# Expert composites from weights split into two FP32R parts: three products in place of one FP32 product, for seven of eight experts

## The chip, the cores and the metric

The kernel runs on one core of a Trainium2 chip. The metric is the device time of one execution, in microseconds (us); smaller is better. TensorE is PE in the rows, VectorE is DVE, ScalarE is ACT, GpSimd is POOL, and SyncE, which issues most DMAs, is SP.

## The reference

The input x has 4 batches of 1024 tokens with 256 features. With xn = layernorm(x):

```python
Q = (x @ Wq.T).reshape(H, b, s, dkh)      # H = 16, dkh = 16; K and V alike
atten = softmax(einsum('hbqd,hbkd->hbqk', Q, K))
out = einsum('hbqk,hbkd->hbqd', atten, V).reshape(b, s, -1)
y = out + x                               # normalised over (1, 2) of each batch
...
logits = xt @ w_gate.T                    # top 2 of 8 experts, softmax of the two
for e in range(E):
    h = xt @ w_in[e].T
    y = y + gates[:, e:e + 1] * (h @ w_out[e].T)
```

The result is x + attention(xn) + experts(xn). There is no nonlinearity between the two products of an expert, so w_out[e] @ w_in[e] can be multiplied first, as one 256x256 matrix. All inputs and the output are FP32.

## The kernel before

Everything is unrolled, each engine has one instruction stream written out by hand, and streams meet only at counting semaphores.

**Composites (first 84 us).** For each of the eight experts `expert_product` (L952) builds the composite matrix of 256x256 from the weights, in two half steps s = 0, 1 of 512 hidden units each. I number the half steps i = 2e + s, from 0 to 15. A half step takes 1 MB of weights: a slot `win[i % 6]` (w_in, 128 partitions x 1024) and a slot `wout[i % 6]` (w_out transposed, the same size). It makes eight products of a 128x128 stationary block with 256 moving columns (two blocks `dh` of the output by four blocks `h` of hidden units) in plain FP32 (L960). The sum stands in PSUM; when both halves of an expert are in, ScalarE (`m_out`, L482) rounds it to FP32R (`mth`) and VectorE (`m_lo`, L667) takes the rest (`mtl`). TensorE may begin expert e only when `m_lo(e - 2)` is done, as banks alternate.

**Work between the composites.** The 32 tiles of tokens come in eight chunks of four tiles. For chunks 0 and 1 TensorE transposes the normalised tokens (`transposes`, L915), and projects values with gate logits (`project_v`, L936) and queries and keys (`project_qk`, L925), in the order of L968 to L993: half steps 0 and 1, transposes(0), half step 2, four `project_v`, two `project_qk`, half step 3, two `project_qk`, half step 4, transposes(1), half step 5, four `project_v`, half step 6, two `project_qk`, half step 7, two `project_qk`, and half steps 8 to 15 with nothing between them. These products already run on operands split in two FP32R parts, three products each. ScalarE empties banks (`xt_out` L489, `v_out` L497, `qk_copy` L517), VectorE takes rests (`xt_lo`, `qk_lo_half`) and computes statistics, GpSimd raises to the power -1/2 (`scale_of_chunk`, L394).

**Loads.** SP issues in one queue (L305 to L320): `load_weights` (L278) for half step i waits until TensorE is done with half step i - 6, whose slot it takes. Ahead of half step 10 stands `qk_out(0)`, eight stores. Slots 2 to 5 are memory that later holds tokens of chunks 4 to 7, so those tokens are loaded after the composites of experts 0 to 5.

**After the composites.** TensorE waits for all sixteen `m_lo` (L1012) and then computes, tile after tile, the products of tokens with composites (`y_bank`, L995), with the rest of the projections between; from about 280 us on the attention follows, up to 985 us, and a short end.

Of the kernel before, what the change touches and what calls it, by code (L numbers as in the profile page):

```python
# [4 lines left out]
FP32 = mybir.dt.float32  # L5
FP32R = mybir.dt.float32r
BF16 = mybir.dt.bfloat16
ALU = mybir.AluOpType
# [3 lines left out]
P = 128  # L12
# [3 lines left out]
def attention_and_experts(nc, x, wq_t, wk_t, wv_t, wg_t, w_in, w_out_t, out):  # L16
    BATCH, S, D = x.shape
# [26 lines left out]
    AHEAD = 8  # L44
    PAIR = 2
    HELD = 4
    SETS = 3
    BY_VECTOR = E // 4

# [8 lines left out]
    with ctx:  # L58
        def sb(name, shape, dt=FP32):
            return ctx.enter_context(nc.sbuf_tensor(name, shape, dt))  # L60

        def sem(name, n=None):
            if n is None:
                return ctx.enter_context(nc.semaphore(name))
            return [ctx.enter_context(nc.semaphore(f"{name}{i}")) for i in range(n)]
# [48 lines left out]
        win = [r.rearrange("p (h d) -> p h d", h=HU) for r in room[0::2]]  # L114
        wout = [r.rearrange("p (h d) -> p h d", h=HU) for r in room[1::2]]
        WS = len(win)
        vb = sb("vb", [P, 2, NKT, VW])
        weights = [picks[:].rearrange("p i t e -> p (i t e)"), vstage[:].rearrange("p t o k v -> p (t o k v)")[:, 0:POS]]
        weights += [wp[:, i, :] for i in (3, 0, 1, 2)]
# [51 lines left out]
        gates_done = sem("gates_done")  # L171
        w_in_s = sem("w_in_s", WS)
        half_done = sem("half_done")
        m_ready = sem("m_ready")
        mh_done = sem("mh_done")
        ml_done = sem("ml_done")
# [96 lines left out]
        def _(sp):  # L273
# [4 lines left out]
            def load_weights(e, s):  # L278

                i = 2 * e + s  # L280
                slot, earlier = i % WS, i - WS
                if earlier >= 0:
                    sp.wait_ge(*((m_ready, KT * (earlier // 2 + 1)) if earlier % 2 else (half_done, earlier // 2 + 1)))
                rows = slice(e * HID + s * HU * P, e * HID + (s + 1) * HU * P)
                for half, w in ((win, w_in), (wout, w_out_t)):
                    sp.dma_start(half[slot], w.rearrange("e h d -> (e h) d")[rows, :]
                                 .rearrange("(p h) d -> p h d", h=HU)).then_inc(w_in_s[slot], 16)
# [94 lines left out]
        def _(pool):  # L382
# [6 lines left out]
            nc.gpsimd.affine_select(out=ident[:], in_=ident[:], compare_op=ALU.not_equal, fill=1.0,  # L389
                                    base=0, pattern=[[-1, P]], channel_multiplier=1).then_inc(const_step, 1)  # L390

            nc.gpsimd.memset(kf[:].bitcast(FP32), 1.0).then_inc(att_const, 1)

            def scale_of_chunk(c):  # L394
                pool.wait_ge(mv_done, 2 * (c + 1))
                nc.gpsimd.tensor_tensor(veps[:], var[:], epst[:, 0:TC], ALU.add).then_inc(veps_done, 1)
                pool.wait_ge(veps_done, c + 1)
                nc.gpsimd.tensor_tensor(rstd[:], veps[:], mhalf[:, 0:TC], ALU.pow).then_inc(rstd_done, 1)

            for c in range(NC // 2):  # L400
                scale_of_chunk(c)

            def add_scaled(t):
                tile = acc[:, bass.ds(t, 1), :].rearrange("p o d -> p (o d)")
# [71 lines left out]
        def _(act):  # L476
# [2 lines left out]
            nc.scalar.copy(wvgh[:], wvg).then_inc(w_hi, 1)  # L479
            nc.scalar.copy(wqkh[:], wqk).then_inc(w_hi, 1)  # L480

            def m_out(e):  # L482

                for dh in range(KT):
                    act.wait_ge(m_ready, KT * e + dh + 1)
                    nc.scalar.copy(mth[:, dh, bass.ds(e, 1), :].rearrange("p o d -> p (o d)"),
                                   ps[:, M_BANK[e % 2][dh], 0:D]).then_inc(mh_done, 1)

            def xt_out(c):  # L489

                if c >= SETS:
                    act.wait_ge(y_ready[-1], TC * (c - SETS + 1))
                for kt in range(KT):
                    act.wait_ge(xt_psum, KT * c + kt + 1)
                    nc.scalar.copy(xth[:, c % SETS, kt, :], ps[:, XT_BANK[kt], :]).then_inc(xth_done, 1)

            def v_out(c, t):  # L497

                if t == 0:
                    act.wait_ge(ones_done, 1)  # L500
                    act.wait_ge(v_stored, 16 * c)
                act.wait_ge(project_ready, 2 * TC * c + t + 1)
                bank = PROJECT_BANK[t % 2]
                nc.scalar.copy(lg[:, TC * c + t, :], ps[:, bank, D:D + E]).then_inc(v_evac, 1)
                nc.scalar.copy(vstage[:, t, :, :, 0:DH], ps[:, bank, 0:D]
                               .rearrange("p (k o d) -> p o k d", o=2, d=DH)).then_inc(v_evac, 1)
                if t == TC - 1:
                    act.wait_ge(v_evac, 2 * TC * (c + 1))
                    act.dma_start(v_d[c * CH:(c + 1) * CH].rearrange("(t p) o f -> p t (o f)", p=P),
                                  vstage[:].rearrange("p t o k v -> p t (o k v)")).then_inc(v_stored, 16)  # L510

            def second_weight(pair):
                act.wait_ge(gap_done, pair + 1)
                rows = slice(PAIR * TC * pair, PAIR * TC * (pair + 1))
                nc.scalar.activation(ex[:, rows], gap[:, rows], ACT.Exp).then_inc(gexp_done, 1)

            def qk_copy(c, o):  # L517
                if o == 0:
                    act.wait_ge(qk_stored, 128 * c)
                act.wait_ge(project_ready, 2 * TC * c + TC + o + 1)  # L520
                nc.scalar.copy(stage[:, 0, o, :].bitcast(FP32R), ps[:, PROJECT_BANK[o % 2], :]).then_inc(qk_hi, 1)  # L521
# [14 lines left out]
                                         ).then_inc(ff_scaled[j - BY_VECTOR], 1)  # L536

            xt_out(0)
            m_out(0)
            for t in range(TC):  # L540
                v_out(0, t)
            for o in range(2):
                qk_copy(0, o)
            m_out(1)
            for o in range(2, 4):
                qk_copy(0, o)
            xt_out(1)
            m_out(2)
            for t in range(TC):
                v_out(1, t)  # L550
            for o in range(2):
                qk_copy(1, o)
            m_out(3)
            for o in range(2, 4):
                qk_copy(1, o)
            m_out(4)
            second_weight(0)
            for e in range(5, E):
                m_out(e)

            for t in range(NT - 1):
                c, i = t // TC + PAIR, t % TC
# [63 lines left out]
        def _(dve):  # L626
# [31 lines left out]
            def xt_lo(c):  # L658

                if c >= SETS:  # L660
                    dve.wait_ge(y_ready[-1], TC * (c - SETS + 1))
                for kt in range(KT):
                    dve.wait_ge(xth_done, KT * c + kt + 1)
                    nc.vector.tensor_tensor(xtl[:, c % SETS, kt, :], ps[:, XT_BANK[kt], :],
                                            xth[:, c % SETS, kt, :].bitcast(FP32), ALU.subtract).then_inc(xtl_done, 1)

            def m_lo(e):  # L667

# [33 lines left out]
            def first_choice(pair):  # L702
                rows = slice(PAIR * TC * pair, PAIR * TC * (pair + 1))
                dve.wait_ge(v_evac, 2 * TC * PAIR * (pair + 1))
                pick(rows, lg, top1, oh1)
# [70 lines left out]
            nc.vector.tensor_tensor(wvgl[:], wvg, wvgh[:].bitcast(FP32), ALU.subtract).then_inc(w_lo, 1)  # L776
            nc.vector.tensor_tensor(wqkl[:], wqk, wqkh[:].bitcast(FP32), ALU.subtract).then_inc(w_lo, 1)
            xt_lo(0)
            m_lo(0)
            token_statistics(1)  # L780
            normalise_tokens(1)
            for o in range(2):
                qk_lo_half(0, o)
            m_lo(1)
            for o in range(2, 4):
                qk_lo_half(0, o)
            xt_lo(1)
            m_lo(2)
            token_statistics(2)
            normalise_tokens(2)  # L790
            for o in range(2):
                qk_lo_half(1, o)
            m_lo(3)
            for o in range(2, 4):
                qk_lo_half(1, o)
            dve.wait_ge(const_step, 6 + E)
            first_choice(0)
            second_choice(0)
            m_lo(4)
            gate_weights(0)  # L800
            token_statistics(3)
            normalise_tokens(3)
            for e in range(5, E):
                m_lo(e)

            for t in range(NT - 1):
                c, i = t // TC + PAIR, t % TC
# [106 lines left out]
        def _(pe):  # L914
# [36 lines left out]

            def expert_product(e, s):  # L952

                slot = (2 * e + s) % WS
                pe.wait_ge(w_in_s[slot], 32 * ((2 * e + s) // WS + 1))
                for dh in range(KT):
                    if s == 0 and e >= 2:
                        pe.wait_ge(ml_done, KT * (e - 2) + dh + 1)
                    for h in range(HU):
                        last = nc.tensor.matmul(ps[:, M_BANK[e % 2][dh], 0:D], win[slot][:, h, dh * P:(dh + 1) * P],  # L960
                                                wout[slot][:, h, :], start=s == 0 and h == 0,
                                                stop=s == 1 and h == HU - 1)
                    if s == 1:
                        last.then_inc(m_ready, 1)
                    elif dh == KT - 1:
                        last.then_inc(half_done, 1)
# [222 lines left out]
```

## Time and profile before

| | us |
|---|---|
| median of three runs | 1004.07 (1003.32 to 1004.2) |
| the profiled execution: its time | 1001.28 |
| its span, first to last instruction | 999.5 |
| PE busy / DVE / ACT / POOL in the span | 974.0 / 780.2 / 694.2 / 285.1 |
| first y product of the second part begins at about | 85.3 |

The span is cut into 40 slices of 25 us in the page; the change touches the first four. A matmul's end is modelled, so what a product costs is read from the distance between starts, not from its duration. The instructions of the change run in the first 85 us; every engine but TensorE is below 60% busy there.

### The profile page before, as it was taken

The page shows a single profiled execution, that of the slowest core. Times are in us where ns is not written, and L with a number is a line of the kernel's source. Part 1 is how long each engine was busy: PE and PEld are TensorE (multiplying, and loading weights), DVE is VectorE, ACT ScalarE, POOL GpSimd, SP SyncE. Part 2 cuts the span into 40 slices and gives each one's busy share as a digit, 9 for nine tenths or more (in the row PEclk, how much of TensorE's full clock was granted, in tenths as well). Part 3 has the DMA queues.
Part 4 walks back from the last instruction along what each step waited for, and adds up shares of the span by engine and source line. Part 5 has one row for each costly group of instructions (what it writes and reads, how often), then busy time and mean ns, then how long its engine had stood idle before and what let it go on. Part 6 is the DMA issues. An engine that isn't in the chain of part 4 may idle for free.

```text
span 999.5 us, 20786 instructions
## 1 busy us (share of the span) xinstructions
PE 974.0 (97%) x7816; PEld 504.5 (50%) x7816; DVE 780.2 (78%) x961; ACT 694.2 (69%) x1385; POOL 285.1 (29%) x389
## 2 busy tenths in 40 slices
PE   7999999999998999999999999999999999999994
PEld 6888888888876433333333333333333333333332
DVE  4344454543466899999999999999999999999975
ACT  2312333333322789999989899898989999899994
POOL 2001445544455222223222322223222322223222
PEclk9999999999999999999999999999999999999997
DMA  9967442223200133333333333333333333332204
GB/s 355 366 248 217 144 139 76 72 78 107 88 23 1 43 98 92 97 92 95 92 93 95 88 100 87 97 92 93 94 91 99 86 98 92 95 93 73 73 23 162
DMA packets 127043, 108.59 MB, mean 109 GB/s; under 512 B 81120, under 2 KB 102368, under 8 KB 126944
## 3 DMA queue, kind: packets, MB, share of 16 engines
q1 hardware_dynamic: 122720, 102.81, 35.4%
q10 hardware_dynamic: 4224, 4.46, 1.3%
q8 instruction: 62, 1.02, 0.4%
q14 instruction: 37, 0.30, 0.1%
HBM read 80.75 MB, written 42.21 MB: 123 GB/s over the span
## 4 chain that ended last, share of the span: by engine, by line
PE 96%; POOL 1%; DMA 1%; DVE 1%; issue 1%; ACT 0%; DVEq 0%; SPq 0%; ACTq 0%; POOLq 0%
PE ps L1081 28%; PE ps L1061 22%; PE ps L1007 18%; PE ps L1039 11%; PE ps L960 6%; PE ps L932 4%; PE ps L948 2%; PE ps L1097 1%; PE ps L1109 1%; PE ps L921 1%; DMA wp<-w_out_t 0%; DMA qf<-ot 0%; POOL rden L425 0%; ACT stage L534 0%; DVE xn L885 0%
## 5 line engine op out<-in xcount | busy, mean ns | idle before, releaser
L750 DVE TENSOR_REDUCE negm<-ps 128x1 f32<-128x1024 f32 x512 | 614.8, 1222 | 31.7 <-PE ps L1039 27.3
L585 ACT ACTIVATE wp<-ps 128x512 f32<-128x512 f32 x680 | 368.9, 595 | 43.7 <-PE ps L1061 6.7
L1061 PE MATMUL ps<-qf,kf 50*128 50x512 f32 x1024 | 373.1, 446 | 0.1
L1039 PE MATMUL ps<-kf,qf 48*128 48x512 f32 x1024 | 366.1, 444 | 1.0 <-DVE negm L750 1.0
L1061 PEld LDWEIGHTS ps<-qf,kf 50*128 50x128 f32 x1024 | 152.6, 185 | 199.0 <-ACT wp L585 97.5
L1081 PE MATMUL ps<-wp,vb 128*17 128x256 f32 x2720 | 212.6, 385 | 0.1
L1039 PEld LDWEIGHTS ps<-kf,qf 48*128 48x128 f32 x1024 | 147.2, 185 | 4.3 <-issue 3.9
L425 POOL TENSOR_TENSOR rden<-choice,minus 128x16 f32<-128x16 f32 x31 | 90.3, 2914 | 151.5 <-ACT choice L604 151.5
L585 ACT ACTIVATE picks<-ps 128x512 f32<-128x512 f32 x172 | 102.7, 597 | 22.8 <-PE ps L1061 5.0
L741 DVE SCALAR_TENSOR_TENSOR acc<-ps,gates,acc 128x256 f32<-128x256 f32 x64 | 30.8, 482 | 101.3 <-PE ps L1007 97.2
L1081 PEld LDWEIGHTS ps<-wp,vb 128*17 128x17 f32 x2720 | 46.0, 95 | 122.7 <-ACT vstage L585 53.2
L440 POOL TENSOR_TENSOR mpart<-negm,zero 128x8 fp32r<-128x8 f32 x64 | 12.9, 201 | 321.3 <-DVE negm L750 321.3
L1007 PE MATMUL ps<-mth,xth 128*128 128x512 f32 x256 | 102.6, 401 | 1.2 <-DVE stage L739 0.5
L585 ACT ACTIVATE vstage<-ps 128x512 f32<-128x512 f32 x172 | 101.8, 592 | 1.1 <-PE ps L1061 1.1
L1007 PE MATMUL ps<-mth,xtl 128*128 128x512 f32 x256 | 101.0, 395 | 0.0
L1007 PE MATMUL ps<-mtl,xth 128*128 128x512 f32 x256 | 100.9, 394 | 0.0
L534 ACT ACTIVATE wp<-ps,gates 128x256 f32<-128x256 f32 x96 | 40.3, 471 | 51.1 <-PE ps L1007 51.1
L521 ACT CAST stage<-ps 128x512 fp32r<-128x512 f32 x32 | 18.8, 587 | 60.2 <-PE ps L932 51.2
L1007 PEld LDWEIGHTS ps<-mth,xth 128*128 128x128 f32 x256 | 48.1, 188 | 14.4 <-issue 4.8
L1081 PE MATMUL ps<-picks,vb 128*17 128x256 f32 x688 | 53.9, 385 | 0.9 <-issue 0.8
L408 POOL TENSOR_TENSOR wp<-wp 128x512 f32<-128x512 f32 x24 | 31.1, 1294 | 82.8 <-ACT wp L534 82.8
L1007 PEld LDWEIGHTS ps<-mth,xtl 128*128 128x128 f32 x256 | 48.1, 188 | 11.5
(124 smaller groups left out, 898.9 us busy)
## 6 DMA issues: line engine op xcount, KB each, us to landing
qk_d<-stage SPq DMA_DIRECT2D x64, 256.0 KB
feat_d<-qk_d SPq DMA_DIRECT2D x64, 256.0 KB, 3.3
qf<-feat_d SPq DMA_DIRECT2D x128, 128.0 KB
qf<-feat_d SPq DMA_DIRECT2D x128, 64.0 KB
kf<-feat_d SPq DMA_DIRECT2D x128, 64.0 KB
v_d<-vstage ACTq DMA_DIRECT2D x8, 544.0 KB, 4.8
vb<-v_d SPq DMA_DIRECT2D x128, 34.0 KB, 2.4
acc<-x SPq DMA_DIRECT2D x8, 512.0 KB, 7.2
```

The costliest lines, as they stand in the source:

```text
L408: nc.gpsimd.tensor_tensor(scaled[:, 0:2], scaled[:, 0:2], scaled[:, 2:4], ALU.add).then_inc(ff_step, 1)
L425: nc.gpsimd.tensor_tensor(rden[:], rows[:, :, :, DH], minus[:], ALU.pow).then_inc(rows_step, 1)
L534: nc.scalar.activation(sums_of(t)[0][:, 2 * (j - BY_VECTOR) + h, :], ps[:, y_bank_of(t, j), h * D:(h + 1) * D], ACT.Copy, scale=gates[:, t ...
L585: nc.scalar.activation(weight_tile(n, j, b)[:, h * HALF:(h + 1) * HALF], ps[:, score_bank(score_turn[unit, b]), :], ACT.Exp).then_inc(exp_ ...
L741: nc.vector.scalar_tensor_tensor(out=total, in0=product, scalar=gate, in1=total, op0=ALU.mult, op1=ALU.add).then_inc(ff_added[j], 1)
L750: nc.vector.tensor_reduce(negm[:, n % 2, qt:qt + 1], ps[:, b:b + 2, :].rearrange("p b c -> p (b c)"), AX.X, ALU.max, negate=True).then_inc ...
L932: last = nc.tensor.matmul(ps[:, PROJECT_BANK[o % 2], :], w[:, o // 2, kt, (o % 2) * P:(o % 2 + 1) * P], v[:, c % SETS, kt, :], start=i == ...
L960: last = nc.tensor.matmul(ps[:, M_BANK[e % 2][dh], 0:D], win[slot][:, h, dh * P:(dh + 1) * P], wout[slot][:, h, :], start=s == 0 and h == ...
L1007: last = nc.tensor.matmul(ps[:, y_bank_of(t, j), :], v[:, t // TC % SETS, kt, tokens], m[:, kt, 2 * j:2 * j + 2, :].rearrange("p e d -> p ...
L1039: last = nc.tensor.matmul(ps[:, MAX_BANK[turn % 2] + half, :], qf[rows, u, qt * P:(qt + 1) * P], kf[rows, u, :], start=True, stop=True)
L1061: nc.tensor.matmul(ps[:, score_bank(score_turn[unit, half]), :], kf[rows, u, j * P:(j + 1) * P], qf[rows, u, h * HALF:(h + 1) * HALF], sta ...
L1081: last = nc.tensor.matmul(ps[32 * c:32 * c + VW, PV_BANK, 0:POS // 4], vb[:, n % 2, j + b * NKT // 2, :], weight_tile(n, j, b)[:, c * (POS ...
```

## The change

Half steps 2 to 15 no longer multiply in FP32. ScalarE rounds both weight slots of a half step to FP32R (`high_of_weights`), GpSimd subtracts the rounded w_in from w_in (`low_of_w_in`), VectorE does so for w_out (`low_of_w_out`). TensorE makes three FP32R products for each one before (high by high, high by low, low by high), 24 in a half step. The split parts stand in two buffers that alternate: `split[0]` is `qf`, `split[1]` is `kf` and the third set of `xth` and `xtl`. So the rounding for half step i waits until TensorE is done with i - 2. A weight slot comes free when its rests are taken. Half steps 0 and 1 stay in FP32. GpSimd's memset of `kf` moves behind the composites. VectorE's statistics of chunk 3, its gate work and its `m_lo` are put in another order, as is GpSimd's `scale_of_chunk`.

```diff
+        flat_kf = kf[:].rearrange("p s k -> p (s k)")
+        split = [[qf[:, i, :] for i in range(4)],
+                 [flat_kf[:, 0:POS], flat_kf[:, POS:2 * POS], xth[:, SETS - 1].rearrange("p k t -> p (k t)"),
+                  xtl[:, SETS - 1].rearrange("p k t -> p (k t)")]]
...
-                if earlier >= 0:
-                    sp.wait_ge(*((m_ready, KT * (earlier // 2 + 1)) if earlier % 2 else (half_done, earlier // 2 + 1)))
+                if 0 <= earlier < WHOLE:
+                    sp.wait_ge(*((m_ready, KT) if earlier else (half_done, 1)))
+                elif earlier > 0:
+                    sp.wait_ge(w_in_low, earlier - WHOLE + 1)
+                    sp.wait_ge(w_out_low, earlier - WHOLE + 1)
...
-            nc.gpsimd.memset(kf[:].bitcast(FP32), 1.0).then_inc(att_const, 1)
...
-            for c in range(NC // 2):
-                scale_of_chunk(c)
+            def low_of_w_in(i):
+                pool.wait_ge(w_high, 2 * (i - WHOLE) + 1)
+                high, low = split[i % 2][0:2]
+                nc.gpsimd.tensor_tensor(low, win[i % WS], high.bitcast(FP32), ALU.subtract).then_inc(w_in_low, 1)
+            scaled_after = {0: 0, 2: 1, 6: 2, 9: 3}
+            for i in range(2 * E):
+                if i >= WHOLE:
+                    low_of_w_in(i)
+                if i in scaled_after:
+                    scale_of_chunk(scaled_after[i])
+            pool.wait_ge(m_ready, KT * E)
+            nc.gpsimd.memset(kf[:].bitcast(FP32), 1.0).then_inc(att_const, 1)
...
+            def high_of_weights(i):
+                slot = i % WS
+                act.wait_ge(w_in_s[slot], 32 * (i // WS + 1))
+                if i >= WHOLE + 2:
+                    act.wait_ge(*((m_ready, KT * ((i - 2) // 2 + 1)) if i % 2 else (half_done, (i - 2) // 2 + 1)))
+                nc.scalar.copy(split[i % 2][0], win[slot]).then_inc(w_high, 1)
+                nc.scalar.copy(split[i % 2][2], wout[slot]).then_inc(w_high, 1)
...
             xt_out(0)
+            high_of_weights(2)
             m_out(0)
             for t in range(TC):
                 v_out(0, t)
+            high_of_weights(3)
             for o in range(2):
                 qk_copy(0, o)
+            high_of_weights(4)
             m_out(1)
             for o in range(2, 4):
                 qk_copy(0, o)
+            high_of_weights(5)
             xt_out(1)
+            high_of_weights(6)
             m_out(2)
             for t in range(TC):
                 v_out(1, t)
+            high_of_weights(7)
...
+            high_of_weights(9)
+            high_of_weights(10)
             m_out(4)
-            second_weight(0)
             for e in range(5, E):
+                high_of_weights(2 * e + 1)
+                if e + 1 < E:
+                    high_of_weights(2 * e + 2)
                 m_out(e)
+                if e == E - 2:
+                    second_weight(0)
...
+            def low_of_w_out(i):
+                dve.wait_ge(w_high, 2 * (i - WHOLE) + 2)
+                high, low = split[i % 2][2:4]
+                nc.vector.tensor_tensor(low, wout[i % WS], high.bitcast(FP32), ALU.subtract).then_inc(w_out_low, 1)
...
+            low_of_w_out(9)
             dve.wait_ge(const_step, 6 + E)
+            token_statistics(3)
+            low_of_w_out(10)
+            m_lo(4)
+            normalise_tokens(3)
+            low_of_w_out(11)
             first_choice(0)
+            low_of_w_out(12)
+            m_lo(5)
             second_choice(0)
-            m_lo(4)
+            low_of_w_out(13)
+            low_of_w_out(14)
+            m_lo(6)
+            low_of_w_out(15)
             gate_weights(0)
-            token_statistics(3)
-            normalise_tokens(3)
-            for e in range(5, E):
-                m_lo(e)
+            m_lo(7)
...
-                slot = (2 * e + s) % WS
-                pe.wait_ge(w_in_s[slot], 32 * ((2 * e + s) // WS + 1))
+                i = 2 * e + s
+                if i < WHOLE:
+                    pe.wait_ge(w_in_s[i], 32)
+                    products = [(win[i], wout[i], h) for h in range(HU)]
+                else:
+                    pe.wait_ge(w_in_low, i - WHOLE + 1)
+                    pe.wait_ge(w_out_low, i - WHOLE + 1)
+                    in_high, in_low, out_high, out_low = split[i % 2]
+                    products = [(a, b, h) for h in range(HU) for a, b in ((in_high, out_high), (in_high, out_low), (in_low, out_high))]
```

The lines left out of VectorE's order put `low_of_w_out(2)` to `(8)` at the places at which ScalarE's order has `high_of_weights(2)` to `(8)`.

## Rows read from the trace of the kernel before

**Rows 1.** The page: busy tenths and granted clock in 40 slices, and the chain by engine.
```profile
PE   7999999999998999999999999999999999999994
...
PEclk9999999999999999999999999999999999999997
...
PE 96%; POOL 1%; DMA 1%; DVE 1%; issue 1%; ACT 0%; DVEq 0%; SPq 0%; ACTq 0%; POOLq 0%
```
**Rows 2.** The chain of waits in order of time, 0 to 100 us: start, us, what.
```profile
6.09 10.02 PE ps L960 x32
...
16.98 3.46 PE ps L960 x16
20.43 3.07 PE ps L948 x24
...
26.36 3.45 PE ps L960 x16
...
55.93 27.64 PE ps L960 x128
...
84.48 1.09 PE ps L921 x8
```
**Rows 3.** Timeline of TensorE, 20 to 24 us: start, us, engine, line, what.
```profile
20.39 0.28 PE L948 MATMUL ps<-wvgl,xth 128*128 128x264 f32 x1
...
21.60 0.28 PE L948 MATMUL ps<-wvgh,xtl 128*128 128x264 f32 x1
```
**Rows 4.** Groups by line and form, 0 to 280 us: busy, mean ns | idle before.
```profile
L408 POOL TENSOR_TENSOR wp<-wp 128x512 f32<-128x512 f32 x24 | 31.1, 1294 | 82.8 <-ACT wp L534 82.8
...
L410 POOL TENSOR_TENSOR wp<-wp 128x256 f32<-128x256 f32 x24 | 17.8, 740 | 1.9
...
L486 ACT CAST mth<-ps 128x256 fp32r<-128x256 f32 x16 | 5.9, 376 | 31.8 <-PE ps L960 31.8
...
L777 DVE TENSOR_TENSOR wqkl<-stage,wqkh 128x1024 fp32r<-128x1024 f32 x1 | 1.2, 1219 | 0.0
L480 ACT CAST wqkh<-stage 128x1024 fp32r<-128x1024 f32 x1 | 1.0, 1040 | 0.0
```
**Rows 5.** Timelines: the tail of the kernel, then 96 to 98 us.
```profile
993.71 0.69 DVE L911 TENSOR_TENSOR stage<-xn,acc 128x512 f32<-128x512 f32 x1
994.08 1.44 POOL L472 TENSOR_TENSOR stage<-xn,acc 128x512 f32<-128x512 f32 x1 [1.19 <-ACT xn L622]
...
994.67 2.00 DVE L911 TENSOR_TENSOR stage<-xn,acc 128x512 f32<-128x512 f32 x2 [0.28 <-ACT xn L622]
...
96.26 1.80 DVE L654 TENSOR_SCALAR xn<-acc,mean,rstd 128x256 f32<-128x256 f32 x4
96.42 0.85 POOL L416 TENSOR_TENSOR acc<-acc,wp 128x256 f32<-128x256 f32 x1
```
**Rows 6.** Lines L911 and L654 alone: duration ns min/median/max.
```profile
L911 DVE TENSOR_TENSOR stage<-xn,acc x3: 678/691/1396, 993.7 to 996.0; 128x512 f32<-128x512 f32 x3
...
L654 DVE TENSOR_SCALAR xn<-acc,mean,rstd x32: 400/407/869, 11.2 to 192.8; 128x256 f32<-128x256 f32 x32
```
**Rows 7.** Timeline of ScalarE at 16 us, of VectorE and GpSimd at 65 us.
```profile
16.58 1.07 ACT L495 CAST xth<-ps 128x512 fp32r<-128x512 f32 x2 [5.26 <-PE ps L921]
...
65.03 1.41 DVE L633 BATCH_NORM_STATS2 st<-acc 128x6 f32<-128x256 f32 x4
...
67.61 1.01 POOL L398 TENSOR_TENSOR rstd<-veps,mhalf 128x4 f32<-128x4 f32 x1
```
**Rows 8.** Timeline of SP's DMA issues, 29 to 40 us: the eight of `qk_out(0)`.
```profile
30.69 8.44 SPq L293 DMA_DIRECT2D qk_d<-stage  x8
```
**Rows 9.** Windows, and PE's last products: us, PE, PEld, DVE, ACT, POOL busy, PEclk, DMA share, GB/s.
```profile
6.09:12.38 6.29, 6.29 (x16) 4.92 (x16) 3.34 (x14) 1.58 (x2) 1.22 (x2) 1.00 1.05 377
...
988.00:989.00 1.00, 0.00 (x0) 0.00 (x0) 0.28 (x1) 0.00 (x0) 0.64 (x1) 0.50 0.44 155
...
984.74 0.66 PE L1097 MATMUL ps<-ident,ot 128*128 128x128 f32 x4 [0.49 <-ACT ot L597]
```

More of the change, by code:

```diff
@@ L46, in attention_and_experts @@
     HELD = 4
+    WHOLE = 2
     SETS = 3
@@ L116, in attention_and_experts @@
         WS = len(win)
+        flat_kf = kf[:].rearrange("p s k -> p (s k)")
+        split = [[qf[:, i, :] for i in range(4)],
+                 [flat_kf[:, 0:POS], flat_kf[:, POS:2 * POS], xth[:, SETS - 1].rearrange("p k t -> p (k t)"),
+                  xtl[:, SETS - 1].rearrange("p k t -> p (k t)")]]
+        split = [[part.rearrange("p (h d) -> p h d", h=HU) for part in parts] for parts in split]
         vb = sb("vb", [P, 2, NKT, VW])
@@ L173, in attention_and_experts @@
         half_done = sem("half_done")
+        w_high = sem("w_high")
+        w_in_low = sem("w_in_low")
+        w_out_low = sem("w_out_low")
         m_ready = sem("m_ready")
@@ L492, in xt_out @@
                     act.wait_ge(y_ready[-1], TC * (c - SETS + 1))
+                elif c == SETS - 1:
+                    act.wait_ge(m_ready, KT * E)
                 for kt in range(KT):
@@ L550, in _ @@
                 v_out(1, t)
+            high_of_weights(7)
             for o in range(2):
                 qk_copy(1, o)
+            high_of_weights(8)
             m_out(3)
@@ L778, in _ @@
             xt_lo(0)
+            low_of_w_out(2)
             m_lo(0)
@@ L781, in _ @@
             normalise_tokens(1)
+            low_of_w_out(3)
             for o in range(2):
                 qk_lo_half(0, o)
+            low_of_w_out(4)
             m_lo(1)
@@ L786, in _ @@
                 qk_lo_half(0, o)
+            low_of_w_out(5)
             xt_lo(1)
+            low_of_w_out(6)
             m_lo(2)
@@ L790, in _ @@
             normalise_tokens(2)
+            low_of_w_out(7)
             for o in range(2):
                 qk_lo_half(1, o)
+            low_of_w_out(8)
             m_lo(3)
@@ L958, in expert_product @@
                         pe.wait_ge(ml_done, KT * (e - 2) + dh + 1)
[L959 to L962, printed above, removed]
+                    for k, (a, b, h) in enumerate(products):
+                        last = nc.tensor.matmul(ps[:, M_BANK[e % 2][dh], 0:D], a[:, h, dh * P:(dh + 1) * P], b[:, h, :],
+                                                start=s == 0 and k == 0, stop=s == 1 and k == len(products) - 1)
                     if s == 1:
```

## The prediction

> **What bounds the kernel now.** I read the page first: TensorE is 90% busy or more in nearly every slice and at full granted clock, and the chain that ends last runs over it for 96% of the span [rows 1]. The chain in order of time shows the part that the change touches: from 6.09 us on TensorE hands over to itself, without a gap, until the composites are done and 84.48 begins the next part [rows 2]. So up to 84.48 us whatever TensorE gains or loses moves the end of the kernel, and since what follows is again bound by TensorE [rows 1], the shift is kept to the end. The question is one number: when does the product at 84.48 start after the change?
>
> **What the change removes.** Eight half steps without anything between them take 27.64 us [rows 2], 3.455 us each. The new half step has 24 FP32R products of 256 columns. The rows have 264 columns: ten starts from 20.39 to 21.60 [rows 3], 0.121 us apiece, so 256/264 of it is 0.1174 and the half step 2.82 us. That is 0.64 us less, fourteen times: **-8.9 us**, if TensorE never waits.
>
> **What it adds, by instruction.** Each of 14 half steps gets two roundings of 128x1024 on ScalarE, 1.04 us each [rows 4], the second begins about 0.93 after the first (two casts of one line overlap by about a tenth [rows 7]); a rest of 128x1024 on VectorE, 1.22 [rows 4]; and one on GpSimd, for which no row has the size. Its 128x256 takes 0.740 and its 128x512 1.294 [rows 4], so 0.554 per 256 more and 1.294 + 2 x 0.554 = **2.40** (I use 2.41). Bounds: 2.2 if the slope falls, 2.6 if twice the 512 row. In busy time this is little: 29 us on ScalarE, 17 on VectorE, 34 on GpSimd, in 80 us. What counts is that they stand in a row before TensorE may start.
>
> **The latency of one half step.** Count from the start of the first rounding. Alone: 1.04, GpSimd 2.41, handoffs 0.1: TensorE may start after **3.55** (VectorE would be done at 1.97 + 1.22, earlier). But the two rests overlap, and both read two SBUF tensors. What that costs shows once in the trace: the L911 that starts at 994.67, while GpSimd's L472 of the same kind runs until 995.52, takes 1.396 instead of 0.691 [rows 5, 6]. It loses 0.705 of an overlap of 0.85, so it goes at 0.16 of its pace, and GpSimd takes 1.44 instead of 1.29, about 0.85 of its pace. The second place agrees in kind: an L654 took 0.869 for 0.407 beside L416 [rows 5, 6]. In the new half step GpSimd starts at 1.07, VectorE at 2.00. GpSimd has 1.48 left, at 0.85 of its pace 1.74, and ends at 3.74; VectorE has done 0.16 x 1.74 = 0.28 by then, its 0.94 left end at 4.68. TensorE starts at **4.72**. I take this value, because its rows are the same instruction on the same engines; 3.55 stays as the lower end.
>
> The Trainium skill, page "GPSIMD Engine Reference", section "Key points", says that GpSimd shares its SBUF interfaces with VectorE, with contention where a VectorE instruction has two SBUF inputs. It gives no size; by it alone the latency would lie somewhere above 3.55.
>
> **The sum, half step by half step.** I went through the four written orders with these durations: a half step starts when TensorE is free and its rests are taken; its rounding when ScalarE is free and half step i - 2 is done. The starts, before and after:
> - Half step 2 was started at 16.98 [rows 2], right behind the transposes. Now ScalarE first rounds the transposes (1.07 from 16.58 [rows 7]), then the weights: 17.65 to 18.1 + 4.72 = 22.8. **+5.8**. Behind it, in TensorE's order, stand the projections of chunk 0, and all that hangs on them.
> - Half step 3: 26.36 before [rows 2]. Its rounding stands behind the last `v_out`, at 29.7, and its VectorE rest has not ended when GpSimd begins the rest of half step 4, whose rounding is free to follow at once. So VectorE is slowed twice over and ends at 36.7. **+10.3**.
> - Half steps 4 to 8 have projections between them (3.07 us for four of `project_v` [rows 2]), which cover most of the latency: the deficit stays between 9.4 and 10.8.
> - Half step 9: +11.3. Half step 10: +14.0, since GpSimd's queue has `scale_of_chunk(3)` ahead of rest 10, and that waits for VectorE's statistics, which now stand behind rest 9; from their start to the end of the power is 65.03 to 68.62 [rows 7], 3.6 us.
> - From half step 11 on nothing is between. An odd half step's rounding waits for the end of half step i - 2 (start + 2.98) and for `m_out` of its second block (0.28 more; one cast is 0.376 [rows 4]). Then 4.72 and 0.1 for the restart: 8.1 us a pair against 6.91 before, +1.2 a pair, half step 15 at 96.9 against 80.1, and the product of 84.48 at 100.7: **+16.2**. The saving of 8.9 is within this sum; it is paid back wholly, as each of the fourteen steps waits for a latency longer than the product it follows.
>
> **The clock.** Two of the waits are long, 5 us each (before half steps 2 and 3). At the tail, TensorE's last products start at 984.74, and in the slice 988 to 989 the granted clock is 0.50, 1.2 GHz [rows 9]. And a start after idleness is dear: the first 16 records take 6.3 us [rows 9] against 3.455 for later ones [rows 2], though the column shows 1.00 there. So after each long wait up to 2.8 us may be lost: 0 to 5.6, I take 3, since part would fall in waits that are there anyway. Together +19.2.
>
> **What costs nothing.** SP's loads: a slot comes free with the rests, and the eight stores of `qk_out(0)`, 8.44 us of issue [rows 8], stand ahead of half step 10 as before; its weights are issued at about 41, by my walk, and needed at 68, so they have over 20 us. The memset of `kf` comes as TensorE starts a part in which `kf` isn't read. If the latency were gone, loads would be next, not now.
>
> The profiled execution took 1001.28, the median is 1004.07; the shift is added to the median: 1004.07 + 19.2 = **1023** rounded.
>
> **The rivals.**
> 1. *The rests don't hinder each other here* (latency 3.55). For it: one wholly overlapped instruction is thin evidence. Against: both rows of it agree. The same walk gives 89.2 for the product of 84.48, +4.7, and one long wait at the clock's price, +0 to 2.8: **1009 to 1012**. Chance 0.17.
> 2. *TensorE is slowed all over*: pauses of 2 to 3 us between products of 2.8 keep the granted clock at 1.2 GHz for stretches. The tail shows that level after a pause [rows 9]; nothing shows it after pauses this short. Another 5 to 10 us: **1028 to 1035**. Chance 0.15.
> 3. *Faster.* The latency hides behind the other half step. Place: the start of odd half steps. A pair costs 3.4 plus the latency, and TensorE needs 5.65, so it decides at a latency of 2.2 us, less than GpSimd's instruction alone; it would need that rest to take about 1.1, as VectorE's does. Then only the wait at half step 2 is left, some 4.4, against 8.9 gained: **999.5**. Chance 0.06.
> 4. *A wash*: rival 1 with a GpSimd of about 1.8 us; within 2 us of before, **1002 to 1006**. Chance 0.05.
>
> The forecast itself, contention as measured and the clock lost at most at two places, has 0.57. The range 1008 to 1032 leaves out faster, wash and the far half of rival 2, about 2 in 10. The least that a measurement of this kernel tells from no change is about 0.2%, 2 us: faster by more 0.06, within it 0.05, slower 0.89.
>
> **What would show it.** In the profile after: FP32R products of L960's successor spaced 0.117 us (right or wrong on the saving); a TensorE wait of over 4 us before half step 2 and before half step 3, released by VectorE's rest; GpSimd's 128x1024 at 2.4 to 2.8; VectorE's rest of 1.22 alone stretched to 2.5 and more in most of 14 cases; pairs of 8.1 us at the end of the composites; the first y product near 101 to 105 instead of 85. The forecast is wrong if VectorE's rest stays at 1.2 (rival 1), if the granted clock shows 0.50 beyond the first 45 us (rival 2), or if TensorE's waits sum to less than 9 us (rivals 3 and 4).

## The result and the profile after

The changed kernel takes 1026.36 us (1025.83 to 1027.25) against 1003.7 of the kernel before on the same chip: ratio **1.0227**, 95% interval 1.0209 to 1.0244, 22.7 us slower. The profiled executions are 1026.5 and 1001.28, 25.2 apart, as the one of before was among its quickest.

The page of the changed kernel, busy tenths and granted clock in 40 slices, and the chain by engine; these answer to [rows 1]:

```profile
PE   4887999999999999999999999999999999999994
...
PEclk9998999999999999999999999999999999999997
...
PE 88%; DVE 3%; DMA 2%; ACT 2%; POOL 1%; issue 1%; SPq 1%; DVEq 0%; ACTq 0%; POOLq 0%
```

All that differs is in the first slices. The chain of waits in order of time (start, us, what) answers to [rows 2]; L1034 is the product that was L960, L510 and L511 are ScalarE's roundings, L717 is VectorE's rest, L414 GpSimd's, L988 the transposes that open the second part:

```profile
17.12 1.07 ACT xth L528 x2
18.20 0.94 ACT qf L510
19.14 0.95 ACT qf L511
20.12 2.54 DVE qf L717
22.79 5.46 PE ps L1034 x24
...
34.73 2.48 DVE xtl L717
37.34 3.12 PE ps L1034 x24
...
79.05 4.65 PE ps L1034 x24
...
98.59 0.94 ACT kf L510
99.53 0.95 ACT xth L511
100.51 2.56 DVE xtl L717
103.21 4.62 PE ps L1034 x24
...
108.73 1.09 PE ps L988 x8
```

Before, the chain through this part was TensorE handing over to itself. Now it goes ScalarE, ScalarE, VectorE, TensorE, again and again, and the transposes that began at 84.48 [rows 2] begin at 108.73, **24.25 us later**. That is nearly the whole of the loss: of the 25.2 us by which the spans differ only 0.95 arise after it.

Starts of the half steps in the trace, and how far each is behind the kernel before:

| half step | before | after | behind | forecast behind, clock apart |
|---|---|---|---|---|
| 2 | 16.98 | 22.79 | 5.8 | 5.8 |
| 3 | 26.36 | 37.34 | 11.0 | 10.3 |
| 8 | 55.93 | 67.0 | 11.1 | 9.4 to 10.8 |
| 9 | 59.4 | 72.41 | 13.0 | 11.3 |
| 10 | 62.8 | 79.05 | 16.2 | 14.0 |
| 15 | 80.1 | 103.21 | 23.1 | 16.8 |
| second part | 84.48 | 108.73 | 24.25 | 16.2 |

**The rests.** VectorE's and GpSimd's instructions in order of time (start, us, engine, what; in brackets the wait before):

```profile
20.12 2.52 DVE L717 TENSOR_TENSOR qf<-xn,qf 128x1024 fp32r<-128x1024 f32 x1 [1.09 <-ACT qf L511]
...
34.73 2.47 DVE L717 TENSOR_TENSOR xtl<-xn,xth 128x1024 fp32r<-128x1024 f32 x1 [6.51 <-ACT xth L511]
...
38.32 2.21 DVE L717 TENSOR_TENSOR qf<-acc,qf 128x1024 fp32r<-128x1024 f32 x1
...
59.88 1.22 DVE L717 TENSOR_TENSOR xtl<-wp,xth 128x1024 fp32r<-128x1024 f32 x1
...
74.31 1.22 DVE L717 TENSOR_TENSOR qf<-acc,qf 128x1024 fp32r<-128x1024 f32 x1
...
88.95 1.75 DVE L761 SCALAR_TENSOR_TENSOR picks<-picks,choice 128x64 f32<-128x64 f32 x1
...
92.11 1.22 DVE L717 TENSOR_TENSOR xtl<-wp,xth 128x1024 fp32r<-128x1024 f32 x1
93.69 2.96 DVE L717 TENSOR_TENSOR qf<-xn,qf 128x1024 fp32r<-128x1024 f32 x1 [0.36 <-ACT qf L511]
```
```profile
19.22 2.34 POOL L414 TENSOR_TENSOR qf<-xn,qf 128x1024 fp32r<-128x1024 f32 x1 [7.52 <-ACT qf L510]
...
36.62 2.83 POOL L414 TENSOR_TENSOR qf<-acc,qf 128x1024 fp32r<-128x1024 f32 x1 [0.50 <-ACT qf L510]
...
74.47 1.11 POOL L406 TENSOR_TENSOR veps<-var,epst 128x4 f32<-128x4 f32 x1 [3.30 <-DVE var L691]
...
88.12 2.50 POOL L414 TENSOR_TENSOR kf<-wp,kf 128x1024 fp32r<-128x1024 f32 x1 [0.85 <-ACT kf L510]
92.78 2.79 POOL L414 TENSOR_TENSOR qf<-xn,qf 128x1024 fp32r<-128x1024 f32 x1 [2.16 <-ACT qf L510]
```

VectorE's rest takes 1.22 us in four of the 14 half steps, where GpSimd is quiet or starts after it, and 2.21 to 2.96 in the ten where it starts into GpSimd's. The one at 20.12 overlaps 1.44 us of GpSimd's run, which ends at 21.56, and then needs 1.08 of its 1.22: it advanced 0.14. The one at 38.32 overlaps 1.13 us and the one at 93.69 1.88, and both again end 1.08 after GpSimd's. So the advance does not grow with the overlap. It works the other way too: GpSimd's addition on four columns, 0.20 us otherwise, takes 1.11 at 74.47, as VectorE's rest has run since 74.31 and ends at 75.53. And GpSimd's rest at 36.62 takes 2.83, since VectorE's from 34.73 ends at 37.20. Whoever starts first keeps nearly its pace, the other all but stands. GpSimd's rest of 128x1024, which I had extrapolated to 2.4, takes 2.34 to 2.42 in ten half steps, and 2.50 to 2.83 in the four where it starts into VectorE's rest or normalisation. L761, the first instruction of `second_choice`, takes 0.215 elsewhere and 1.75 here, as GpSimd's rest has run since 88.12; VectorE's rest of half step 13 stands behind it.

**The clock.** Windows of the changed kernel: from:to us, length, then PE, PEld, DVE, ACT, POOL busy (instructions), granted clock, DMA share, GB/s:

```profile
23.00:26.00 3.00, 3.00 (x15) 3.00 (x16) 2.33 (x11) 0.00 (x0) 0.41 (x2) 0.50 1.06 383
...
73.55:76.50 2.95, 2.95 (x15) 2.95 (x15) 2.20 (x9) 0.37 (x1) 1.95 (x2) 0.50 0.87 329
83.90:86.50 2.60, 2.60 (x24) 2.58 (x22) 1.26 (x4) 2.13 (x3) 1.61 (x1) 1.00 0.00 0
94.00:97.00 3.00, 3.00 (x17) 3.00 (x15) 3.00 (x2) 0.37 (x1) 1.57 (x1) 0.50 0.68 245
```

TensorE is busy in all four, but only 15 to 17 products fall in some 3 us at 0.50, 1.2 GHz, and 24 in 2.6 us at 1.00; in the timeline they start 0.213 us apart at the one and 0.12 at the other. From their first start to the end of the row of starts, half steps 2, 9, 10, 13 and 15 take 5.26, 4.44, 4.53, 4.44 and 4.44 us where 2.95 is the price at full clock.

### The profile page after: what moved, and what is told of

The parts are those of the page before. It is cut to its first block, busy times and chain, and to the rows that moved or that the text cites. A ratio compares the mean times of both kernels' runs of the same rounds, so it can differ in the third digit from the quotient of the medians.

```text
span 1024.7 us, 21098 instructions
## 1 busy us (share of the span) xinstructions
PE 976.1 (95%) x7928; PEld 511.4 (50%) x7928; DVE 815.9 (80%) x975; ACT 720.9 (70%) x1413; POOL 320.4 (31%) x403
## 4 chain that ended last, share of the span: by engine, by line
PE 88%; DVE 3%; DMA 2%; ACT 2%; POOL 1%; issue 1%; SPq 1%; DVEq 0%; ACTq 0%; POOLq 0%
PE ps L1154 27%; PE ps L1134 21%; PE ps L1080 17%; PE ps L1112 11%; PE ps L999 4%; PE ps L1034 3%; PE ps L1015 2%; DMA qf<-ot 2%; PE ps L1182 1%; PE ps L1170 1%; DMA wp<-w_out_t 1%; DVE qf L717 1%; DVE xtl L717 1%; PE ps L988 1%; POOL rden L447 0%
## 5 line engine op out<-in xcount | busy, mean ns | idle before, releaser
L1154 PE MATMUL ps<-vstage,vb 128*17 128x256 f32 x688 | 53.9, 385 | 0.0
```

The costliest lines, as they stand in the source:

```text
L1154: last = nc.tensor.matmul(ps[32 * c:32 * c + VW, PV_BANK, 0:POS // 4], vb[:, n % 2, j + b * NKT // 2, :], weight_tile(n, j, b)[:, c * (POS ...
```

## The experiments

The theory after the result: three costs, one upon the other. (1) The chain of rounding and rests is longer than the products that could cover it. (2) The two rests hinder each other, which makes the chain 4.7 us instead of 3.5. (3) The waits lower TensorE's clock. The rivals: one of the three does it all; or the moved work does. Each ratio is against runs of the kernel before on the same chip, whose median lay between 1003.99 and 1004.82.

**e1: VectorE's rest cut to 8 of 1024 columns.**

```diff
-nc.vector.tensor_tensor(low, wout[i % WS], high.bitcast(FP32), ALU.subtract)
+nc.vector.tensor_tensor(low[:, 0, 0:8], wout[i % WS][:, 0, 0:8], high[:, 0, 0:8].bitcast(FP32), ALU.subtract)
...
-for a, b in ((in_high, out_high), (in_high, out_low), (in_low, out_high))
+for a, b in ((in_high, out_high), (in_high, out_high), (in_low, out_high))
```

> Left out: VectorE takes the rest of only 8 of the 1024 columns of w_out, and the product high by low uses the high part of w_out in its place; TensorE's work, GpSimd's rest and all waits stay. Theory (the two rests share a way to SBUF, so that VectorE's rest stands almost still while GpSimd's runs and then ends 1.1 us after it; and long waits cost clock): the latency from rounding to product falls from 4.6 to 3.5 us, the first y product comes at 91 to 94 us instead of 108.7, the time is 1010 to 1013. Rival (VectorE's 2.5 us is not what sets the end; the row rounding, GpSimd, TensorE is): at most 1 us less than the changed kernel, 1025 to 1027. Rival (clock alone): 1016 to 1019, as shorter waits would keep the clock.

Measured: 1015.52 us (1013.47 to 1017.37), ratio 1.0102 (1.0075 to 1.0129): 1.25% under the changed kernel. Second part at 97.68. That is later than the 91 to 94 expected; 2.2 us of it arise before half step 2, mainly as half step 1, plain FP32, took 5.4 us in this execution and not 3.7. The rival that VectorE's 2.5 us do not set the end falls. The clock alone does not fall here: 1015.52 lies between the 1010 to 1013 of the theory and the 1016 to 1019 of that rival, and the saving holds clock too, as only half steps 2 and 10 are still slow (about 4.4 and 4.3 us).

**e2: both rests on VectorE.** With its rests gone from GpSimd's queue, `scale_of_chunk` no longer stands between any of them, as in the kernel before.

```diff
-nc.gpsimd.tensor_tensor(low, win[i % WS], high.bitcast(FP32), ALU.subtract).then_inc(w_in_low, 1)
+nc.vector.tensor_tensor(low, win[i % WS], high.bitcast(FP32), ALU.subtract).then_inc(w_in_low, 1)
```

> Both rests go to VectorE, w_in first; GpSimd takes none. Nothing is left out. Theory of sharing: each rest takes 1.22 us again, the latency is 1.04 + 1.22 + 1.22 = 3.5 us, first y product at 91 to 93, time 1010 to 1013, equal to e1 within 2 us. Rival (VectorE's rest takes 2.5 us by itself in this place, for its tiles or for the DMA beside it): two of them make the latency 6 us and the time 1035 or more. Either way slower than before, since the chain is still longer than the 2.8 us of products that could cover it.

Measured: 1013.75 (1012.98 to 1015.9), ratio 1.0093 (1.0073 to 1.0113); second part at 93.83. The two lines of rests, each with count, ns min/median/max, first and last start:

```profile
L707 DVE TENSOR_TENSOR kf<-xn,kf x3: 1225/1225/1226, 31.2 to 87.3; 128x1024 fp32r<-128x1024 f32 x3
```
```profile
L710 DVE TENSOR_TENSOR xtl<-xn,xth x3: 1217/1217/1219, 32.3 to 88.4; 128x1024 fp32r<-128x1024 f32 x3
```

Nothing of 2.5 us is left: the longest of all 28 takes 1.226. One engine doing both rests one after the other is faster by 1.34% (1.0227 less 1.0093), 13 us, than two doing them at once. Both the time and the second part come just behind what was expected (1010 to 1013, 91 to 93). Its waits remain (engine, line waited for: us in all, times, longest), 4.2 us before half step 2 and 7.6 in six others:

```profile
PE ps L1027 <- DVE xtl L710: 7.6, 6, 1.7
...
PE ps L1027 <- DVE qf L710: 4.2, 1, 4.2
```

**e3: the changed kernel with the waits filled.**

```diff
+FILL = {2: 20, 3: 20, 9: 16, 10: 12, 12: 10, 13: 12, 15: 14}
+for _ in range(FILL.get(i, 0)):
+    if i == 2:
+        nc.tensor.matmul(ps[:, PROJECT_BANK[0], 0:P], ident[:], ident[:], start=True, stop=True)
+    else:
+        nc.tensor.matmul(ps[:, XT_BANK[1], 0:D], wvgh[:, 0, 0:P], wvgh[:, 1, 0:D], start=True, stop=True)
```

> TensorE gets products that nobody reads, put ahead of the waits of half steps 2 (20 of FP32, 128 columns), 3 (20), 9 (16), 10 (12), 12 (10), 13 (12) and 15 (14), FP32R of 256 columns, each group shorter than the wait it stands in. All else as in the changed kernel. Theory (the granted clock falls in the waits, and the products after them cost 1.6 to 2.6 us more in five half steps): granted clock 1.00 throughout, first y product 5 to 9 us earlier than 108.7, time 1017 to 1021. Rival (the waits are set by the other engines alone, and a slow product only fills a wait that would be there anyway): 1025 to 1027.

Measured: 1021.5 (1020.38 to 1023.16), ratio 1.0168 (1.0147 to 1.0188), 0.59% under the changed kernel and half a us above the 1017 to 1021 expected, though TensorE does 124 more records. Windows over three half steps that were slow, columns as above:

```profile
22.80:25.90 3.10, 3.10 (x26) 3.10 (x27) 2.54 (x12) 0.00 (x0) 0.30 (x2) 1.00 1.05 383
69.78:72.90 3.12, 3.12 (x26) 3.12 (x27) 3.02 (x12) 0.37 (x1) 1.06 (x1) 1.00 0.69 234
...
99.05:102.16 3.11, 3.11 (x24) 2.90 (x24) 1.44 (x6) 0.37 (x1) 0.00 (x0) 1.00 0.57 211
```

Half steps 2, 9 and 15 run at full clock in 3.1 us, and the second part begins at 103.08, 5.65 earlier. The five slow half steps cost 8.4 us in products together, so some 3 us of that lay in waits that come back. So the clock is worth about 6 us here, and is not the whole loss. From half step 11 to 13 it still takes 9.81 us:

```profile
80.97 0.36 PE L1041 MATMUL ps<-xth,kf 128*128 128x256 f32 x1 [1.42 <-DVE xtl L717]
...
90.78 0.36 PE L1041 MATMUL ps<-xth,kf 128*128 128x256 f32 x1 [0.90 <-DVE xtl L717]
```

**e4: the statistics of chunk 3 earlier.**

```diff
+            token_statistics(3)
             low_of_w_out(9)
-            token_statistics(3)
...
-            scaled_after = {0: 0, 2: 1, 6: 2, 9: 3}
+            scaled_after = {0: 0, 2: 1, 6: 2, 8: 3}
```

> VectorE's statistics of chunk 3 stand ahead of its rest 9 instead of behind it, and GpSimd's scale of chunk 3 follows rest 8. Theory: half step 10 no longer waits for it, 2 to 3 us less, 1023 to 1024.5. Rival: the statistics then delay the rest of half step 9 by as much: no change, 1026. If the clock is the larger matter, one wait less can save 4 us.

Measured: 1037.24 (1035.77 to 1038.1), ratio 1.0322 (1.0302 to 1.0342): 11 us slower than the changed kernel, outside all that I expected. GpSimd and VectorE in this run:

```profile
71.10 1.12 POOL L406 TENSOR_TENSOR veps<-var,epst 128x4 f32<-128x4 f32 x1 [6.27 <-DVE var L691]
72.29 1.01 POOL L408 TENSOR_TENSOR rstd<-veps,mhalf 128x4 f32<-128x4 f32 x1
73.27 2.74 POOL L414 TENSOR_TENSOR kf<-xn,kf 128x1024 fp32r<-128x1024 f32 x1
...
96.35 2.39 POOL L414 TENSOR_TENSOR kf<-wp,kf 128x1024 fp32r<-128x1024 f32 x1 [8.12 <-ACT kf L510]
```
```profile
96.46 2.36 DVE L750 TENSOR_TENSOR picks<-picks,rank 128x64 f32<-128x64 f32 x1
...
99.45 3.37 DVE L717 TENSOR_TENSOR xtl<-wp,xth 128x1024 fp32r<-128x1024 f32 x1
```

GpSimd's rest of half step 9 now stands behind the scale and starts at 73.27, not at 68.80, so the wait moved one half step ahead. Further on, a VectorE instruction on 64 columns, 0.23 us otherwise, lies 2.36 us under GpSimd's rest, and VectorE's rest takes 3.37 between two of GpSimd's. The second part begins at 118.01. With two queues that block each other a harmless-looking order is not harmless; which of these makes how much of the 11 us I did not separate.

**e5: the moved work without the split.** `WHOLE` gives way to `SPLIT`, which names the half steps that are split; here none, and all go the FP32 way. From here on the two buffers alternate over the half steps named.

```diff
-    WHOLE = 2
+    SPLIT = ()
```

> No half step is split: all sixteen in FP32 as before, but with every other part of the change, the moved statistics, gate work, scale and memset. Theory (all of the loss is in the split): the time of before within 1 us. Rival (the moves cost by themselves): 2 us or more slower than before.

Measured: 1004.0, ratio 1.0002 (0.9993 to 1.0012). The moves cost nothing; all of the loss is in the split.

**e6 and e7: fewer half steps split.** The same edit with `SPLIT` holding 4 to 15, and 4 to 8.

> Half steps 2 and 3 stay in FP32 too, 4 to 15 are split as in the changed kernel, with GpSimd's rest. Theory (5.8 us of the loss come at half step 2 and 4.5 more at 3, where nothing covers the rounding and the clock falls; the rest in the last seven): the deficit up to half step 8 vanishes, the first y product comes at 90 to 94, time 1009 to 1013. Rival (the start is made good by waits later): 1020 or more.

> Only half steps 4 to 8 are split, those that have projections between them, with both GpSimd's and VectorE's rests. Theory: latency of 4.6 us is mostly covered by 2.8 of products and 2.9 of projections, five times 0.64 are gained less some 2 of waits: 0 to 2 us faster than before. Rival (the sharing or ScalarE's queue delays half steps even here): 2 to 4 us slower.

Measured: e6 1016.42, ratio 1.0126 (1.0111 to 1.014); second part at 97.81. It loses 10 us less than the changed kernel, but not as much as expected (1009 to 1013, second part at 90 to 94): half step 1 again took 5.4 us, and half steps 9, 10 and 12 took about 4.4, 4.5 and 4.2 us, in part or wholly at low clock. e7 1003.69, ratio 1.0 (0.9987 to 1.0013), at the edge of the 0 to 2 us gained that were expected. Here TensorE still waits 2.4 us, in half steps 5 and 7, for VectorE's rest beside GpSimd's:

```profile
PE ps L1042 <- DVE xtl L725: 2.4, 2, 1.5
```

**e8: split only where a cover exists, rests on VectorE.** `SPLIT = (4, 5, 6, 7, 8, 10, 12, 14)` and the edit of e2.

> Split are half steps 4 to 8 and then 10, 12 and 14, each with an FP32 half step of 3.45 us ahead of it, and VectorE takes both rests. Latency 3.5 us, cover 3.45 us or more everywhere, and two buffers, so that it should be hidden: eight times 0.64 gained, less waits of under 1 us: 3.5 to 5 us faster than before, 999 to 1001. Rival (a latency is left over in each, or VectorE's own queue is too full with 2.4 us of rests a half step): within 1 us of before.

Measured: 1001.5 (999.47 to 1004.66), ratio **0.9978** (0.9964 to 0.9991), a little faster than before; second part at 81.58. TensorE's waits on rests are down to this:

```profile
PE ps L1035 <- DVE xtl L718: 0.4, 1, 0.4
```

I expected 3.5 to 5 us and got 2.2 in the runs, 2.9 in the trace. A half step among others costs 2.95 and not 2.82 (the change of product type and the first product after it), so eight give 4.0. The wait takes 0.4 of it and the projections behind half step 7 0.3 (3.05 us where others take 2.79). That leaves the 3.35 us by which the stretch from the first transposes to the second part is shorter than before (16.39 to 81.58 against 15.94 to 84.48); the trace's 2.9 has lost 0.45 more before that stretch.

**e9: e2 with the waits filled**, as in e3, with {2: 15, 3: 12, 9: 8, 10: 8, 11: 10, 13: 10, 15: 8}.

> e2 (both rests on VectorE) with products that nobody reads ahead of the waits of half steps 2 (15 of FP32, 128 columns), 3 (12), 9 (8), 10 (8), 11 (10), 13 (10) and 15 (8), each group shorter than its wait. This leaves the bare chain of rounding and rests. Theory (three parts: chain, sharing, clock): 2 to 4 us less than e2, 1009.5 to 1011.5. Rival (without the sharing the waits are too short to cost clock beyond the first): 1 us less than e2 or nothing.

Measured: 1011.0 (1009.92 to 1012.86), ratio 1.0065 (1.005 to 1.008), as expected; second part at 92.50. This is the bare chain.

**e10: e8 with half step 3 split as well.**

```diff
-    SPLIT = (4, 5, 6, 7, 8, 10, 12, 14)
+    SPLIT = (3, 4, 5, 6, 7, 8, 10, 12, 14)
...
             xt_out(0)
-            high_of_weights(2)
+            high_of_weights(3)
...
             xt_lo(0)
-            low_of_w_out(2)
+            low_of_w_out(3)
```

> e8 with half step 3 split too, its rounding and rests put where the changed kernel has those of half step 2. They have from 17.7 to 26.4 us, so they are covered: 0.6 us less than e8, 0.3 to 0.45% faster than before. Rival: ScalarE's two roundings delay m_out(0) and the first v_out, or VectorE's rests the statistics of chunk 1, and the gain is lost: as e8 or 1 us slower.

Measured: 1000.48 (999.72 to 1001.59), ratio **0.9959** (0.9944 to 0.9973), within what was expected. It has the lowest ratio, 4.1 us under the kernel before, but its interval overlaps that of e8, and the traces don't support that half step 3 adds to it: from the first transposes to the second part e10 takes 65.88 us (16.43 to 82.31) and e8 65.19. In its trace a new wait of 1.1 us stands before a `project_qk`, whose bank VectorE empties late:

```profile
PE ps L998 <- DVE stage L732: 1.1, 1, 1.1
```

## Why the prediction was right, and where it was off

The forecast was 1023 in 1008 to 1032, slower with 0.89; it came out 1026.4. By its steps:

- **The latency: right.** 4.72 was forecast from the start of the first rounding to TensorE's first product. In the trace it is 18.08 to 22.79, 32.63 to 37.34 and 98.49 to 103.21: 4.71, 4.71 and 4.72. That it fits to 0.01 is luck: at half step 2 VectorE's rest ended 4.56 after the start and not 4.68, and the handoff took 0.15 and not 0.04. Where other work stands in a queue it is longer, 6.47 at half step 13.
- **The sharing: right**, shown by the timeline and e2, with e1 and e7 in line. Its picture was off: I treated it as a mutual slowing in proportion, and it is nearer to a turn that the first keeps. The second advances 0.14 us whether it waits 1.13 or 1.88, and my own row says the same: L911 advanced 0.14 in 0.85 us. L472's 0.15, which I put down to the L911 behind it, has a likelier cause in front: it started at 994.08, while the L911 before it ran until 994.40. In the changed kernel GpSimd's rest, ahead of VectorE's, kept its 2.34.
- **The saving: right in kind.** Products are 0.12 us apart; a half step takes 2.95, 0.13 more than my 2.82.
- **Half step 3: right by two errors.** I had VectorE's rest slowed twice over and ending at 36.7. It was slowed once, since the rest of half step 4 came too late to hinder it. But its rounding began at 32.63 instead of 29.7, behind a half step and projections at low clock. The two nearly cancel.
- **Half step 10: right.** It lost a further 3.2 us, 2.7 forecast, waiting for GpSimd behind the scale of chunk 3. From the start of the statistics to the end of the power it took 4.5 us and not 3.6, as GpSimd's addition stood 0.9 under VectorE's rest.
- **The clock: the term that was mis-sized.** I took 3 us, at no more than the two long waits. It fell at the first of them, did not at the second (1.00 at half step 3), and fell again at half steps 9, 10, 13 and 15, after waits of 1.9 to 2.4 us that I had held too short. Ratios 1.0227 and 1.0168 (e3) give 5.9 us. This is rival 2's mechanism, and the sign I had named for it, 0.50 beyond 45 us, did show, so the clock term of the forecast was wrong by its own sign; the rival's price of 5 to 10 on top of the rest was too high. So the truth lies between forecast and rival 2.
- **The pairs at the end** took 9.9 and 9.7 us, not 8.1, for two reasons. From half step 13 to 15 (93.47 to 103.21) it is the clock: half step 13 took 4.44 for 2.95. From 11 to 13 (83.58 to 93.47) it is not, as both half steps of the pair ran at 1.00 and e3 still takes 9.81. There it is the sharing once more, at a place that my walk left out: `second_choice` stands ahead of VectorE's rest of half step 13, took 3.2 us (88.95 to 92.11) with L761 under GpSimd's rest, and 1.6 in e9, where GpSimd has none.
- **The signs.** TensorE's waits in the part sum to 20.9 us, far over 9, and the one before half step 2 was 5.3; but the one before half step 3 was 2.8 and not over 4, as TensorE came free 3 us later than in my walk and VectorE's rest ended only 0.5 later. The first y product came at 109.6, not at 101 to 105.

The Trainium skill's page "GPSIMD Engine Reference", section "Key points", had named the sharing for VectorE instructions with two SBUF inputs. The trace agrees and gives the size, 1.30 us lost of 1.44 overlapped.

The 22.7 us by experiment, each part as a difference of two ratios to before:

| part | from | us | by the traces, first transposes to second part |
|---|---|---|---|
| bare chain longer than its cover, less the saving | e9: 1.0065 | 6.5 | 7.5 |
| the two rests in each other's way | e3 less e9: 1.0168 - 1.0065 | 10.3 | 10.5 |
| clock | changed kernel less e3: 1.0227 - 1.0168 | 5.9 | 5.6 |
| moved work | e5: 1.0002 | 0 | 0 |

By the intervals of the ratios the first part is known to some 1.5 us, the second and third to some 2.5 each; the traces' stretches (68.54 before, 92.24 changed, 86.61 e3, 76.08 e9, 68.55 e5) agree. The forecast had 4.7, 11.5 and 3.0. The parts depend on the order in which they are taken: without sharing the clock costs 2.8 (e2 less e9). And the second is not sharing alone: taking the rests from GpSimd also frees half step 10 of the scale ahead of its rest, and from half step 9 to 10 it takes 6.64 us in e3 and 4.35 in e9. How much of these 2.3 us is the order in the queue was not separated.

## What to carry to other kernels

Judge work put ahead of a busy TensorE by the length of its chain against the work that can run meanwhile, not by busy time: here 29, 17 and 34 us on three half-idle engines lost 22.7 us on the fourth, and the split in the places that have a cover, with both rests on VectorE, gained 2 to 4. Two elementwise instructions on SBUF operands, one for VectorE and one for GpSimd, are not parallel work: both on VectorE took 2.4 us, both at once 3.4 (19.22 to 22.64). And a chain of short waits can cost the clock as well. The mean over the kernel hardly shows it (0.984 against 0.994), the granted clock of a window around the products does.

## What the runs showed that I had not expected

- A VectorE instruction that reads one SBUF tensor, with a mean and a factor per token, and nothing of PSUM was held as long as one that reads two: a normalisation of 256 columns (L700), 0.407 us in the median, took up to 2.498 beside GpSimd's rest. `m_lo` (L723), which reads PSUM and one SBUF tensor, was never above 0.425, and two of them ran from 88.28 on, under GpSimd's rest.

```profile
L700 DVE TENSOR_SCALAR xn<-acc,mean,rstd x32: 398/407/2498, 11.7 to 217.0; 128x256 f32<-128x256 f32 x32
```
```profile
L723 DVE TENSOR_TENSOR mtl<-ps,mth x16: 407/412/425, 22.6 to 108.2; 128x256 fp32r<-128x256 f32 x16
```

- A wait of 2.8 us of TensorE before half step 3 left the granted clock at 1.00, one of 2.4 before half step 9 was followed by 0.50 from 73.5 us on. The length of a wait alone did not tell. Why the clock fell at the one and not at the other stays open.
- Half step 1, equal in all kernels, took 3.7 us in most profiled executions and 5.4 in those of e1 and e6, before anything that the kernels differ in: the granted clock from 13.5 to 15.5 us was 0.55 and 0.52 there, and 1.00 over that half step before and after the change. Two us of a single trace's first 20 are chance; compare the start of the part in question, not only its end.
